# A graph layer that sorts its edges on the chip: the ranks are added up on TensorE, routing runs one pair later, and the constant row is added per quad

## What is computed

```python
h_self = x @ W_lin + b_lin
messages = x[col] @ W_msg + b_msg          # row, col = src, dst
msg_sum = segment_sum(messages, row)
counts = segment_sum(ones, row)
h_agg = msg_sum / maximum(counts, 1.0)[:, None]
h = relu(concatenate([h_self, h_agg], axis=1) @ W_upd + b_upd)
out = layernorm(x + h)
```

## Time and profile before

| | us |
|---|---|
| median of 3 runs | 1657.13 |
| lowest, highest | 1656.5, 1659.34 |
| the profiled execution | 1663.77 |
| its span | 1662.0 |
| granted clock, mean over the span | 0.876 |

### The profile page before, as it was taken

How to read it: one execution, slowest core, us unless ns; L and a number is a source line. 1 busy time by engine, 2 the same in 40 slices (tenths; PEclk the granted TensorE clock), 3 DMA queues, 4 the chain that set the end, 5 groups by cost and what they waited for, 6 DMA issues and landing times.

```text
span 1662.0 us, 42934 instructions
## 1 busy us (share of the span) xinstructions
PE 1352.0 (81%) x16656; PEld 829.0 (50%) x16656; DVE 1131.1 (68%) x2880; ACT 783.1 (47%) x1128; POOL 474.1 (29%) x512
## 2 busy tenths in 40 slices
PE   2868757667766279999999999999999999999997
PEld 2858757667666134444444444444444444444443
DVE  7999899999999425555555555555555555555554
ACT  1222213100010136666666666666666666666664
POOL 1000000000000244444444444444444444444430
PEclk9777768655555579999999999999999999999998
DMA  6222222132000353443434444444444444444420
GB/s 89 84 84 99 72 76 88 55 111 62 4 1 1 121 147 100 118 118 117 119 118 119 119 117 120 119 117 119 119 119 119 118 118 118 119 119 118 120 51 11
DMA packets 119790, 160.60 MB, mean 97 GB/s; under 512 B 32099, under 2 KB 91552, under 8 KB 119516
## 3 DMA queue, kind: packets, MB, share of 16 engines
q1 hardware_dynamic: 95426, 110.08, 20.1%
q0 software_dynamic: 22880, 47.02, 12.8%
q10 hardware_dynamic: 1290, 0.78, 0.2%
HBM read 134.62 MB, written 23.21 MB: 95 GB/s over the span
## 4 chain that ended last, share of the span: by engine, by line
PE 55%; DVE 31%; ACT 7%; issue 6%; DMA 1%; DVEq 0%; ACTq 0%; SPq 0%
PE slot L1233 30%; PE acc L1247 16%; ACT big L539 7%; DVE big L777 5%; DVE big L757 5%; DVE big L782 3%; DVE big L788 3%; PE acc L1258 2%; PE slot L1283 2%; DVE big L815 2%; PE acc L1266 2%; DVE big L808 2%; DVE big L784 2%; PE slot L1274 1%; DVE big L814 1%
## 5 line engine op out<-in xcount | busy, mean ns | idle before, releaser
L539 ACT ACTIVATE big<-slot 128x768 bf16<-128x768 f32 x850 | 649.7, 810 | 405.7 <-PE slot L1233 359.9
L1233 PE MATMUL slot<-big 128*128 128x384 bf16 x2900 | 553.0, 329 | 67.2 <-ACT big L539 46.9
L1233 PEld LDWEIGHTS slot<-big 128*128 128x128 bf16 x2900 | 244.1, 98 | 353.6 <-issue 177.5
L625 POOL DMA_INDIRECT big<-x,dst_at x300 | 292.2, 974 | 288.9 <-PE acc L1247 173.6
L1247 PE MATMUL acc<-big 32*128 32x385 bf16 x6800 | 352.5, 325 | 0.0
L929 DVE TENSOR_TENSOR big<-col_lo,iota_lo 128x512 bf16<-128x512 f16 x425 | 179.6, 423 | 239.7 <-PE acc L1247 226.0
L629 POOL DMA_INDIRECT big<-x,sp_i x175 | 175.7, 1004 | 286.6 <-PE acc L1266 135.7
L919 DVE TENSOR_SCALAR big<-big,iota_k 128x512 bf16<-128x512 f16 x725 | 228.9, 351 | 23.4 <-PE slot L1233 12.0
L1143 PE MATMUL acc<-big 125*100 125x64 f16 x1600 | 132.7, 260 | 118.3 <-DVE big L815 118.3
L1247 PEld LDWEIGHTS acc<-big 32*128 32x128 bf16 x6800 | 141.0, 93 | 175.6 <-issue 101.3
L1143 PEld LDWEIGHTS acc<-big 125*100 125x100 f16 x1600 | 127.7, 185 | 125.8 <-DVE big L815 125.8
(11 more groups left out here) (151 smaller groups left out, 1141.9 us busy)
## 6 DMA issues: line engine op xcount, KB each, us to landing
big<-rows SPq DMA_DIRECT2D x25, 2176.0 KB
x<-big SPq DMA_DIRECT2D x19, 480.0 KB, 2.8
big<-x SPq DMA_DIRECT2D x32, 192.0 KB, 2.4
big<-in_x SPq DMA_DIRECT2D x24, 256.0 KB
big<-base SPq DMA_DIRECT2D x24, 256.0 KB
out<-big SPq DMA_DIRECT2D x24, 256.0 KB
big<-in_x SPq DMA_DIRECT2D x19, 320.0 KB, 3.5
base<-big SPq DMA_DIRECT2D x19, 320.0 KB, 2.2
```

Of the source, the lines that this page charges most:

```text
L539: act.activation(xg[n % NX][:, :, 0:F3], slot[z % 2][:, :, 0:F3], ACT.Copy).then_inc(s["xg_ready"], 1)
L625: pool.indirect_dma_start(out=xg_d[:, c, 0:F3], out_offset=None, in_=x3_dram, in_offset=bass.IndirectOffsetOnAxis(ap=dst_at[:, q, c:c + 1] ...
L1233: ins = nc.tensor.matmul(slot[z % 2][:, j, 0:F3], W[R_ % NW_][:, k, (c % 4) * P:(c % 4 + 1) * P], xwin[:, win_at(c) + k, :], start=k == 0, ...
```

## The change

Three things are changed.

**The ranks.** VectorE no longer adds Qf up over hi by itself. `route` is cut in two: `pick(u)` is the multiplication that writes Qf (L786 of the changed kernel, L777 before), and a new function `add_ranks(u)` on TensorE (L1156) multiplies Qf by the identity in 20 matmuls of 200 columns that all add into one PSUM tile Q_ps, each with five of the 100 values of hi. VectorE then reduces Q_ps, 200 numbers a partition, to 40 (L796), in place of L782, L784 and L788. Q_ps shares its PSUM bank with T_ps.

**The order.** `route(u)`, from the reduce on, stands one pass later: VectorE runs `pick(u)`, `test_hi(u + 1)`, `route(u - 1)`. TensorE runs `fill_bins(u - 1)`, `add_ranks(u)`, `count_before(u + 1)`, then the work on x. ScalarE's `take_T` moves one pass later too. OH has 4 buffers.

**The constant row.** `make_base` no longer adds it (five f32 matmuls with their weight loads less for each of 20 blocks). A copy of the row on all partitions, `const_rep`, is made once, and `add_constant` adds it to base4 by one more VectorE instruction of 128 x 512 in f32 for each quad. The making of that row (`b_lin_w`, two matmuls over 128 rows in place of one, a wider ScalarE copy) is left out of the diff below.

```diff
@@ -120,7 +120,7 @@
 
 
         one_a = Area(NWIN_A * F3 * 2, WIN_BYTES + AREA_BYTES)
-        OH = [shaped(one_a.take(2 * T * H, f16), "p (a h j) -> p a h j", h=H, j=2) for _ in range(3)]
+        OH = [shaped(one_a.take(2 * T * H, f16), "p (a h j) -> p a h j", h=H, j=2) for _ in range(4)]
         OHSV = [shaped(one_a.take(2 * T * 2 * SL, f16), "p (a v n j) -> p a v n j", v=2, n=SL, j=2) for _ in range(2)]
         one_b = one_a
         Qf = one_b.take(2 * T * H, f16)
@@ -221,12 +222,15 @@
...
+        NH = 5
+        Q_ps = [acc[2 + b][0:EP, 0:T * NH * 2] for b in range(2)]
         R_ps = [acc[b][0:EP, 0:2 * H] for b in range(2)]
         T_ps = [acc[2 + b][0:H, 0:4 * SL] for b in range(2)]
@@ -519,12 +523,14 @@
                     cast_hi(u)
                 if u < XB:
                     cast_mid(u)
-                take_T(u)
+                if u > 0:
+                    take_T(u - 1)
                 if u < XB:
                     take_base(u)
                 for k in range(NS - 1):
                     if u == US * (k + 1) + 1:
                         keep_slab(k)
+            take_T(U - 1)
             keep_slab(NS - 1)
 
             act.wait_ge(s["flag_known"], 1)
@@ -752,9 +759,9 @@
                 return a.unsqueeze(1).to_broadcast([a.shape[0], pairs, a.shape[1], 2])
 
             def test_hi(u):
-                if u >= 3:
-                    dve.wait_ge(s["T_made"], u - 2)
-                nc.vector.tensor_tensor(OH[u % 3][0:EP, :, :, :], spread2(two_chunks(hi, u), H), tbl(iota2h[0:EP, :, :]), ALU.is_equal).then_inc(s["OH_ready"], 1)
+                if u >= 4:
+                    dve.wait_ge(s["T_made"], u - 3)
+                nc.vector.tensor_tensor(OH[u % 4][0:EP, :, :, :], spread2(two_chunks(hi, u), H), tbl(iota2h[0:EP, :, :]), ALU.is_equal).then_inc(s["OH_ready"], 1)
 
             def split_1(b):
                 dve.wait_ge(s["hi_cast"], b + 1)
@@ -769,24 +776,25 @@
                 x3b = x_blk[b % 2][0:n, :].rearrange("p (j f) -> p j f", f=F)
                 nc.vector.tensor_tensor(x3_blk[b % 2][0:n, :, 2 * F:F3], x3b, x3_blk[b % 2][0:n, :, F:2 * F], ALU.subtract).then_inc(s["lo_made"], 1)
 
-            def route(u):
+            def pick(u):
 
                 b = u % 2
                 dve.wait_ge(s["R_taken"], u + 1)
+                if u > 0:
+                    dve.wait_ge(s["Q_added"], u)
                 n = Qf[0:EP, :].rearrange("p (k a e) -> p k a e", k=2, a=TP)
-                nc.vector.tensor_tensor(n, OH[u % 3][0:EP, :, :, :].rearrange("p (k a) h j -> p k a (h j)", k=2),
+                nc.vector.tensor_tensor(n, OH[u % 4][0:EP, :, :, :].rearrange("p (k a) h j -> p k a (h j)", k=2),
                                         R16[b][0:EP, :, :, :].rearrange("p k h j -> p k (h j)").unsqueeze(2).to_broadcast([EP, 2, TP, 2 * H]),
                                         ALU.mult).then_inc(s["Q_made"], 1)
-                dve.wait_ge(s["Q_made"], u + 1)
-                Q3 = Qf[0:EP, :].rearrange("p (a e) -> p a e", e=2 * H)
-                k = mark(nc.vector.tensor_tensor(Q3[:, :, 0:H], Q3[:, :, 0:H], Q3[:, :, H:2 * H], ALU.add))
-                after(k)
-                k = mark(nc.vector.tensor_tensor(Q3[:, :, 0:H // 2], Q3[:, :, 0:H // 2], Q3[:, :, H // 2:H], ALU.add))
-                after(k)
+
+            def route(u):
+
+                b = u % 2
+                dve.wait_ge(s["Q_added"], u + 1)
                 r2 = red[0:EP, :].rearrange("p (a j) -> p a j", j=2)
                 with nc.allow_low_precision("whole numbers below 2501 in fp16; 64 and over are told apart"):
-                    k = mark(nc.vector.tensor_reduce(r2, Q3[:, :, 0:H // 2].rearrange("p a (h j) -> p a j h", j=2), AX.X, ALU.add))
-                after(k)
+                    nc.vector.tensor_reduce(r2, Q_ps[b].rearrange("p (a h j) -> p a j h", h=NH, j=2), AX.X, ALU.add).then_inc(s["ranks_taken"], 1)
+                dve.wait_ge(s["ranks_taken"], u + 1)
                 k2 = r_all[0:EP, 2 * u:2 * u + 2, :].rearrange("p c (a j) -> p (c a) j", j=2)
                 k = mark(nc.vector.tensor_tensor(k2, r2, two_chunks(dupc, u), ALU.add))
                 after(k)
@@ -851,11 +859,13 @@
             prepare(0)
             test_hi(0)
             for u in range(U):
+                pick(u)
                 if u + 1 < U:
                     test_hi(u + 1)
                 if 0 < u <= XB:
                     split_2(u - 1)
-                route(u)
+                if u > 0:
+                    route(u - 1)
                 if u < XB:
                     split_1(u)
                 if u == 3:
@@ -869,6 +879,7 @@
                         decode(k)
                     if u == US * (k + 1) + 2:
                         spill_values(k)
+            route(U - 1)
             decode(NS - 1)
             spill_values(NS - 1)
             dve.wait_ge(s["sv_made"], NS)
@@ -967,6 +978,8 @@
                 def add_constant(q):
                     dve.wait_ge(s["S_ready"], q + 1)
                     dve.wait_ge(base4_loaded[q % 2], 16 * (q // 2 + (2 if q == Q - 1 else 1)))
+                    k = mark(nc.vector.tensor_tensor(base4[q % 2], base4[q % 2], const_rep.unsqueeze(1).to_broadcast([P, 4, F]), ALU.add))
+                    after(k)
                     for h in range(4):
                         ins = nc.vector.scalar_tensor_tensor(out=base4[q % 2][:, h, :], in0=bmsg_rep, scalar=cnt[:, 2, h:h + 1], in1=base4[q % 2][:, h, :],
                                                              op0=ALU.mult, op1=ALU.add)
@@ -1129,18 +1142,27 @@
                 for k in range(2):
                     for a in range(TP):
                         for j in range(2):
-                            ins = nc.tensor.matmul(R_ps[u % 2][:, k * H:(k + 1) * H], tri16[0:EP, 0:EP], OH[u % 3][0:EP, k * TP + a, :, j],
+                            ins = nc.tensor.matmul(R_ps[u % 2][:, k * H:(k + 1) * H], tri16[0:EP, 0:EP], OH[u % 4][0:EP, k * TP + a, :, j],
                                                    start=a + j == 0, stop=a + j == TP)
                 ins.then_inc(s["R_made"], 1)
 
-            def fill_bins(u):
-                pe.wait_ge(s["route_ready"], u + 1)
+            def add_ranks(u):
+
+                pe.wait_ge(s["Q_made"], u + 1)
                 if u >= 2:
                     pe.wait_ge(s["T_taken"], u - 1)
+                of = Qf[0:EP, :].rearrange("p (a e) -> p a e", e=2 * H)
+                for h in range(0, H, NH):
+                    ins = nc.tensor.matmul(Q_ps[u % 2], ident16[0:EP, 0:EP], of[:, :, 2 * h:2 * (h + NH)], start=h == 0, stop=h == H - NH)
+                ins.then_inc(s["Q_added"], 1)
+
+            def fill_bins(u):
+                pe.wait_ge(s["ranks_taken"], u + 1)
+                pe.wait_ge(s["route_ready"], u + 1)
                 for k in range(2):
                     for a in range(TP):
                         for j in range(2):
-                            ins = nc.tensor.matmul(T_ps[u % 2][:, k * 2 * SL:(k + 1) * 2 * SL], OH[u % 3][0:EP, k * TP + a, :, j], OHSV[u % 2][0:EP, k * TP + a, :, :, j],
+                            ins = nc.tensor.matmul(T_ps[u % 2][:, k * 2 * SL:(k + 1) * 2 * SL], OH[u % 4][0:EP, k * TP + a, :, j], OHSV[u % 2][0:EP, k * TP + a, :, :, j],
                                                    start=a + j == 0, stop=a + j == TP)
                 ins.then_inc(s["T_made"], 1)
 
@@ -1175,26 +1197,27 @@
                 n = xb_rows(b)
                 for j in range(XJ):
                     o = slot[1][0:n, j // 4, j % 4 * F:(j % 4 + 1) * F]
-                    nc.tensor.matmul(o, xT_blk[:, j * P:j * P + n], A, start=True, stop=False)
-                    ins = nc.tensor.matmul(o, ones[:, 0:n], const_pad[:, :], start=False, stop=True)
+                    ins = nc.tensor.matmul(o, xT_blk[:, j * P:j * P + n], A, start=True, stop=True)
                 ins.then_inc(s["base_made"], 1)
 
             pe.wait_ge(s["iota_cast"], 2)
             count_before(0)
             pe.wait_ge(s["w_taken"], 1)
             for u in range(U):
+                if u > 0:
+                    fill_bins(u - 1)
+                add_ranks(u)
                 if u + 1 < U:
                     count_before(u + 1)
                 if u < XB:
                     if u == US + 2:
                         pe.wait_ge(s["lo_taken"], 1)
                     turn_x(u)
-                fill_bins(u)
-                if u < XB:
                     make_base(u)
                 for k in range(NS - 1):
                     if u == US * (k + 1) + 1:
                         lay_slab(k)
+            fill_bins(U - 1)
             lay_slab(NS - 1)
 
             pe.wait_ge(s["flag_ready"], 1)
```

More of the change, by code:

```diff
@@ L206, in gnn_program @@
         w_T = sb("w_T", [P, 2, P], f32)
-        AB = sb("AB", [P, 3, F], f32)
-        A, B, bmsg_rep = AB[:, 0, :], AB[:, 1, :], AB[:, 2, :]
+        AB = sb("AB", [P, 4, F], f32)
+        A, B, bmsg_rep, const_rep = [AB[:, i, :] for i in range(4)]
```

(22 more changed lines are left out.)

4 lines of the change are left out of this document (removed).

## The result

The changed kernel took 1925.23 us (median of 4 runs, 1924.13 to 1926.74) against 1658.24 us of the kernel before (median of 4, measured beside it): a ratio of 1.161, 95% interval 1.159 to 1.163. It is slower by 267 us, on the forecast's side and inside the range of 1800 to 1960, 45 us above the 1880 that was named. The profiled execution has a span of 1922.6 us, 260.6 more than before.

The account below looks back on a forecast made before the run. VectorE bounded stage one before; afterwards VectorE and TensorE alternate, 8.0 + 0.6 + 9.5 = 18.1 us a pass. The loop takes 729 against 506.7 us, 222 more: 1886 from the profiled 1663.8, median 6.6 lower, 1880; range 1800 to 1960.

Parts of the forecast that it names:

- The turns: Main loop: VectorE's whole pass, then filling, adding and counting on TensorE, then ScalarE's copy, one after another; 222 us more.
- A late pass: Main-loop pass without work on x: VectorE 8.0, copy with handovers 0.6 and TensorE 9.5, together 18.1 us.
- TensorE's part: Filling, adding and counting in one main-loop pass: 11.3 us at 1.2 GHz, 9.5 with the clock rising within the burst.
- The passes with work on x: Main-loop passes 1 to 20, with `split_2` in them: 0.74 us above 18.1, so 18.84 us each.
- Nothing of these overlaps except `split_1` and the work between passes: Main loop: only these run beside the alternating engine parts; `prepare` with `split_1`, 9.2 us, fits VectorE's idle 10 us.
- Were it not covered, 25 us more: Main loop: the addition if `prepare`, 8.45 us and three times on the path before, did not run in VectorE's idle time.
- The clock: TensorE in the main loop: each burst begins at 1.2 GHz and rises 7.0 us in, making its part 9.5 us.
- cold throughout: Rival, chance 0.14: TensorE's clock rises only as a burst ends; 1.8 us more in 38 passes, 1948 us.
- full clock: Rival, chance 0.07: TensorE's clock, once up, outlasts VectorE's part; 3.2 us less in 38 passes, 1758 us.
- The edits at nothing: Covered `prepare`, decoding and spills, the 100 f32 matmuls gone from `make_base`, and stage two's 0.69 us add: no cost.
- Slow reads: Rival, chance 0.06: reading Qf in pieces of ten columns doubles the adding, 2 to 3.5 us a pass; 1960 to 2010.
- the turns don't bind, and it is faster: Rival, chance 0.04: VectorE's next pass finds R ready, each pass is 2.9 us shorter, 116 in all; 1541 us.

Follow-up runs that it names:

- The fillers: The changed kernel with 76 matmuls of 200 columns, whose result nobody reads, behind count_before(u + 1) in passes 21 to 38: 1863.87 us, ratio 1.153.

## Why the prediction was right, and where it was off

**The turns: right.** That counting behind the filling makes the two engines alternate was shown from three sides: taking it away ends the loss (0.945), putting it alone into the old kernel makes the loss (1.138), and more work between the two is paid in full (2.5 us a late pass).

**A late pass: right, a little high.** Foretold 18.1, measured 17.95 in the pass shown and 17.7 as a mean (pass 20's pick at 455.1 to pass 39's at 790.7, 19 passes). VectorE's part was put at 8.0 and is 8.1, the reduce from PSUM 0.36 and is 0.36, the twenty matmuls 3.5 and are 3.5 at 1.2 GHz. TensorE's part was 9.5 in the forecast and is 9.3 here; the clock rose a little earlier than 7.0 us in (0.99 from 576 to 577, and the burst began at 569.28).

**The passes with work on x: wrong by 55 us, and this is the whole miss.** The step that failed is "Nothing of these overlaps except `split_1` and the work between passes". `split_1` did not overlap. I had looked at what it costs and not at what it waits for: `cast_hi`, queued on ScalarE behind the copy of R. These passes have 20.5 us (422.8 for the first 20, less 10.6 for pass 0 and 23 for two prepares, a decode and a spill, over 19) in place of 18.84, which makes 31 of the 55 us. The other 23 are the work between passes: with `split_1` late, `prepare` (twice 8.45 us), a decode and a spill came after TensorE's part too, though they were said to be covered. From the first pick to that of pass 20 the forecast has 368 us (10.2 + 19 x 18.84), and the trace 422.8 (32.35 to 455.1): 55 more. From there to the last filling it has 361 (18.84 + 18 x 18.1 + 16.4), and the trace 352.4 (455.1 to 807.57): 9 less. Together 46 more, and the median lay 45 above the forecast. Taking `cast_hi` and `turn_x` out of the queue gave 56 us back. The prediction had a part of this in view ("Were it not covered, 25 us more") and gave it no place in its range: 1800 to 1960 was made wide for the clock and the adding. That it holds the result in spite of this term is in part luck.

**The clock: right in kind.** Each burst began at 1.2 GHz and rose within it. Of the rivals, neither *cold throughout* nor *full clock* came true. The fillers show that the full clock saves some 3 us a pass, and that most of the loss would stay. In the late pass shown, filling began after 8.68 us of idle and took 3.64 us, where 2.04 were measured behind the fillers. The Trainium skill (TensorE: Matmul & The Clock Gate, "HAM oscillation — how this bites in real kernels") tells of bursts that start slow again after each wait, and the trace agrees with it.

**The edits at nothing: right.** The constant row by itself moved nothing (0.9993). *Slow reads* did not come true: twenty matmuls that read Qf in pieces of ten columns took what their columns cost.

**The rival on the other side** (*the turns don't bind, and it is faster*, 1541) was rightly held unlikely for this order, and it is what the same change does in another: 1527 and 1495 us, on chips where the kernel before takes 1616.

## What to carry to other kernels

When work moves by one step of a software pipeline, write down for each engine what stands ahead of the instruction that the next step waits for; a static queue turns "needs A and stands behind B" into "needs A and B", and in the kernel before that alone cost 14%. On each engine put first what another engine waits for soonest, and last what waits for the latest input. When you call an instruction hidden, check what it waits for as well as what it costs, on the third engine too.

## What the runs showed of the hardware that was not expected

TensorE's clock fell some 2 us into a burst that had begun at 2.4 GHz at 568.53 us, after 6.7 us of fillers, 2.1 us of idling and a filling (granted 1.00 from 569 to 570, 0.77 from 570 to 571, 0.50 from 572 to 573). In the next pass the same rows came after the same idling, and the clock stayed up: filling 2.04 us, adding 1.92, counting 2.48. Two measurements of the same kernel that agree in stage one to a microsecond (826.2 and 827.0 us at its end) differ by 39 us in stage two.
